# Handing out expert pages inside the graph network's loop, with scatters to fixed pages, in a graph and mixture kernel

## The reference, cut to what matters

```python
    xn = _layernorm(x, axis=-1)
    x = x + gnn(xn, edge_index, edge_attr_64, ...) + mix(xn, ...)
    z = _layernorm(x, axis=-1)
    # the experts, on z (256 wide; the hidden width H is 64)
    logits = z @ router_w.T + router_b
    idx = argmax(logits, axis=-1)
    h = relu(einsum('nd,ndh->nh', z, W1[idx]) + b1[idx])
    return x + relu(einsum('nh,nhd->nd', h, W2[idx]) + b2[idx])
```

## Time and profile before

| | |
|---|---|
| median of 3 runs | 2876.47 us |
| profiled execution, own time | 2884.98 us |
| its span, first to last instruction | 2883.2 us |
| mean granted TensorE clock | 0.956 |
| busy: TensorE, its weight loads | 2631.6 us (91%), 2462.9 us (85%) |
| busy: VectorE, ScalarE, POOL | 2143.3 us (74%), 1581.4 us (55%), 1756.9 us (61%) |
| moved by DMA | 207.99 MB, mean 72 GB/s |

### The profile page before, as it was taken

How to read it: one execution, slowest core, us unless ns; L and a number is a source line. 1 busy time by engine, 2 the same in 40 slices (tenths; PEclk the granted TensorE clock), 3 DMA queues, 4 the chain that set the end, 5 groups by cost and what they waited for, 6 DMA issues and landing times.

```text
span 2883.2 us, 57776 instructions
## 1 busy us (share of the span) xinstructions
PE 2631.6 (91%) x19546; PEld 2462.9 (85%) x19546; DVE 2143.3 (74%) x4892; ACT 1581.4 (55%) x3080; POOL 1756.9 (61%) x1614
## 2 busy tenths in 40 slices
PE   5889999999989999998999999899999998993497
PEld 3667899999989999997999999799899998993365
DVE  8988677777767777776777777788888886894055
ACT  0545476666636666664666666444444445671165
POOL 2045587777778777777877776555555553224566
PEclk7999999999999999999999999999999998996699
DMA  6022322222242232224222222343333322201343
GB/s 127 29 49 55 96 64 68 64 58 61 51 116 60 61 69 59 64 45 118 60 64 64 65 59 51 94 120 89 86 89 87 93 75 57 62 26 39 83 116 94
DMA packets 255570, 207.99 MB, mean 72 GB/s; under 512 B 165506, under 2 KB 194387, under 8 KB 255278
## 3 DMA queue, kind: packets, MB, share of 16 engines
q1 hardware_dynamic: 197678, 162.55, 21.8%
q0 software_dynamic: 57600, 41.75, 7.3%
HBM read 136.93 MB, written 70.16 MB: 72 GB/s over the span
## 4 chain that ended last, share of the span: by engine, by line
PE 59%; DVE 15%; POOL 11%; issue 9%; ACT 2%; DVEq 1%; DMA 1%; SPq 0%; ACTq 0%; POOLq 0%; another core or an unknown queue 0%
PE bank L399 54%; POOL edges_sorted L787 7%; PE bank L1918 4%; DVE hidh_lo L1394 3%; POOL tokens_sorted L853 2%; DVE xh L1358 2%; DVE scr L1268 1%; DVE oh L1591 1%; DVEq L1570 1%; PE bank L2381 1%; POOL ehl L803 1%; DVE bn L1349 1%; POOL r L765 1%; DMA queries<-qn 1%; DVE res L1366 1%
## 5 line engine op out<-in xcount | busy, mean ns | idle before, releaser
L787 POOL DMA_INDIRECT edges_sorted<-staging,pos_i x850 | 1075.7, 1265 | 246.4 <-issue 229.8
L910 ACT ACTIVATE hid<-bank,b1p 128x250 f32<-128x250 f32 x800 | 331.5, 466 | 319.3 <-PE bank L399 286.3
L399 PE MATMUL bank<-w_hi,hidh_hi 128*125 128x256 f32 x1600 | 472.2, 295 | 23.1 <-DVE hidh_lo L1394 22.9
L399 PE MATMUL bank<-h_hi,w_hi 128*128 128x250 f32 x1600 | 479.1, 299 | 3.7 <-DVE h_lo L1378 3.4
L399 PE MATMUL bank<-w_hi,hidh_lo 128*125 128x256 f32 x1600 | 453.7, 284 | 0.0
L1394 DVE TENSOR_TENSOR hidh_lo<-hid,hidh_hi 128x500 fp32r<-128x500 f32 x400 | 319.7, 800 | 178.6 <-ACT hidh_hi L916 145.7
L399 PE MATMUL bank<-w_lo,hidh_hi 128*125 128x256 f32 x1600 | 452.2, 283 | 0.0
L399 PE MATMUL bank<-h_hi,w_lo 128*128 128x250 f32 x1600 | 448.5, 280 | 0.0
L399 PE MATMUL bank<-h_lo,w_hi 128*128 128x250 f32 x1600 | 445.0, 278 | 0.0
L399 PEld LDWEIGHTS bank<-w_hi,hidh_hi 128*125 128x125 f32 x1600 | 300.8, 188 | 32.1 <-DVE hidh_lo L1394 29.3
L399 PEld LDWEIGHTS bank<-h_hi,w_hi 128*128 128x128 f32 x1600 | 303.9, 190 | 8.4 <-DVE h_lo L1378 6.1
(11 more groups left out here) (292 smaller groups left out, 6625.5 us busy)
## 6 DMA issues: line engine op xcount, KB each, us to landing
staging<-edges_sorted SPq DMA_DIRECT2D x103, 260.0 KB
staging<-in_edge_attr SPq DMA_DIRECT2D x50, 531.2 KB
queries<-qn SPq DMA_DIRECT2D x100, 250.0 KB
qin<-queries SPq DMA_DIRECT2D x100, 250.0 KB
edges_sorted<-staging,pos_i POOLq DMA_INDIRECT x850
rows_in<-edges_sorted SPq DMA_DIRECT2D x50, 260.0 KB
yin<-tokens_sorted SPq DMA_DIRECT2D x81, 127.0 KB
raw<-in_L_mix_W SPq DMA_DIRECT2D x8, 1024.0 KB, 5.6
```

The lines of the kernel that those rows point to most:

```text
L399: return nc.tensor.matmul(o, left, right, start=start, stop=stop, skip_group_check=True)
L787: nc.gpsimd.indirect_dma_start(out=edges_sorted, out_offset=bass.IndirectOffsetOnAxis(ap=pos_i[:, i:i + 1], axis=0), in_=stage[:, slot, j, ...
L910: a = nc.scalar.activation(hid[c % 2][:, j, :], chunks(PH[c % 2])[:, j, :], ACT.Gelu, bias=b1p[:, 2 * c + j:2 * c + j + 1])
```

## The change

The table of sorted tokens becomes 80 pages of 128 rows (`PAGE`), and each page belongs to one expert. Pages are handed out as the groups come: for every group the kernel counts how many tokens of each expert there are so far, opens a new page for an expert whose last one is full, and gives each token of the group a row. POOL scatters the group's two tiles at once, in the graph loop.

- `rank_tokens(g)` on TensorE, first in pass `g + 7`: three to five small products of `chosen` (now bf16, in two buffers) with triangles and ones, summed in `PQT` over all groups. It waits for `chosen` of the group, the last instruction of VectorE's pass before, and for `n_counted` of the group before.
- On VectorE nine instructions more for group `i-7` in pass `i`, between the others: `route_rank` (two), `route_pages` (two), `route_ends` (a scan), `route_grown`, `route_book`, `route_pick` (256 columns) and `route_sum` (a reduce over 320 columns). `route_count` and the old rank (four instructions) go.
- On POOL `token_slots(i-8)`, nine small instructions, and `scatter_tokens(i-8)`, two indirect DMAs, at the end of pass `i`. The loops become one pass longer on TensorE and VectorE, and four on POOL.
- Since rows of a page may stay unused, all 80 pages are written beforehand: in passes 0 to 19 of the first layer SP issues three transfers each (`fill_pages`), which put any finite values and the row number 25000 there, which the scatter of the results skips. They stand behind `load_queries` and ahead of what SP issues for the rest of the pass.
- The position arithmetic and the table of segments go. SP reads the experts of the pages back with one load (`page_kind`), and loads page after page from addresses fixed in the program, with no register. `omiss` goes. 24 idle products stand ahead of the expert loop, before its wait for the table.
- Buffers: the bf16 helpers of the edge sort (`tri16` and its like) lie in a place of `hid[1]` now. Two small memsets come to the set-up of constants, and five VectorE instructions in place of one ahead of the graph loop.

The diff, cut to its core:

```diff
-IDLE_SCATTER = 48
+IDLE_LOAD = 24
...
+PAGE = 128
+PAGE_RND = 8388608.0 * PAGE
+FILL = 4
+FSEGS = (N + EXP * (PAGE - 1)) // PAGE
...
-    tokens_sorted = nc.dram_tensor("tokens_sorted", (N, YROW), F32, kind="Internal").ap()
+    tokens_sorted = nc.dram_tensor("tokens_sorted", (FSEGS * PAGE, YROW), F32, kind="Internal").ap()
...
+        chosen = [sb(f"chosen{i}", [P, PAIR, EXP], BF16) for i in range(2)]
+        tri_r = sb("tri_r", [128, 128], BF16)
+        ones_r = sb("ones_r", [128, 128], BF16)
+        rest_r = sb("rest_r", [128, 128], BF16)
...
+            def fill_pages(t):
+                rows = tokens_sorted[t * FILL * PAGE:(t + 1) * FILL * PAGE, :].rearrange("(k p) c -> p k c", p=PAGE)
+                for k in range(KC):
+                    sp.dma_start(rows[:, :, k * 128:(k + 1) * 128], tri[:, :].unsqueeze(1).to_broadcast((PAGE, FILL, 128))).then_inc(blank_written, 16)
+                sp.dma_start(rows[:, :, D:YROW], unused[:, :].unsqueeze(1).to_broadcast((PAGE, FILL, YROW - D))).then_inc(blank_written, 16)
...
+                if l == 0 and t == 0:
+                    sp.wait_ge(consts, NCONST)
+                if l == 0 and 0 <= t < FSEGS // FILL:
+                    fill_pages(t)
...
-            sp.wait_ge(r_table, 2)
+            sp.dma_start(page_kind[:, :, :], tokens_sorted.rearrange("(k p) c -> p k c", p=PAGE)[0:1, :, D:YROW]).then_inc(blank_written, 16)
             for n in range(FSEGS):
-                first = sp.value_load(ffirst_i[0:1, n:n + 1], min_val=0, max_val=N - P)
                 if n >= YIN:
                     sp.wait_ge(f_row, n - YIN + 1)
-                    sp.wait_ge(f_idx, 2 * (n - YIN + 1))
-                sp.dma_start(yin[n % YIN][:, :], tokens_sorted[bass.ds(first, P), :]).then_inc(tokens_in(n)[0], 16)
+                    sp.wait_ge(f_idx, n - YIN + 1)
+                sp.dma_start(yin[n % YIN][:, :], tokens_sorted[n * PAGE:(n + 1) * PAGE, :]).then_inc(tokens_in(n)[0], 16)
...
+            nc.gpsimd.memset(unused[:, :], 0.0).then_inc(consts, 1)
+            pool.wait_ge(consts, 6)
+            nc.gpsimd.memset(unused[:, 2:3], float(4 * N)).then_inc(consts, 1)
...
+            def token_slots(g):
+                old, new = g % 2, (g + 1) % 2
+                pool.wait_ge(n_placed, g + 1)
+                of_kind = picked[:, g % 2, :, :]
+                rank, late, more = of_kind[:, :, 4], slots[:, 2, :], slots[:, 3, :]
+                for k in range(2):
+                    own_step(nc.gpsimd.tensor_tensor(slots[:, k, :], of_kind[:, :, 2 * k], of_kind[:, :, 2 * k + 1], ALU.subtract))
+                own_step(nc.gpsimd.tensor_tensor(late, rank, of_kind[:, :, 2 * old + 1], ALU.subtract))
+                pool.wait_ge(p_step, own[0])
...
+                own_step(nc.gpsimd.tensor_copy(fpos_i[:, PAIR * g:PAIR * (g + 1)], slots[:, 5, :]))
+                SLOTTED[g] = own[0]
+                pool.wait_ge(p_step, own[0])
+
+            def scatter_tokens(g):
+                for t in range(PAIR * g, PAIR * (g + 1)):
+                    nc.gpsimd.indirect_dma_start(
+                        out=tokens_sorted, out_offset=bass.IndirectOffsetOnAxis(ap=fpos_i[:, t:t + 1], axis=0),
+                        in_=res[:, t, :], in_offset=None).then_inc(f_scat, 16)
+
+            for i in range(GROUPS + 8):
                 if i < GROUPS:
                     pool.wait_ge(N_IN[i % 2], 16 * (i // 2 + 1))
                     nc.gpsimd.tensor_tensor(pair(res, i), pair(res, i), x_in[i % 2][:, :, :], ALU.add).then_inc(n_x, 1)
-                if i >= 4:
+                if 4 <= i < GROUPS + 4:
                     pool.wait_ge(n_ve, i - 3)
                     nc.gpsimd.tensor_tensor(pair(res, i - 4, D + 1)[:, :, D], gve[:, :], tail_half[:, :], ALU.pow).then_inc(n_root, 1)
-
-            pool.wait_ge(f_posi, 1)
-            for t in range(TILES):
-                nc.gpsimd.indirect_dma_start(
-                    out=tokens_sorted, out_offset=bass.IndirectOffsetOnAxis(ap=fpos_i[:, t:t + 1], axis=0),
-                    in_=res[:, t, :], in_offset=None).then_inc(f_scat, 16)
-                if t == TILES - 4:
-                    nc.gpsimd.memset(tail_half[:, :], -0.5).then_inc(f_ones, 1)
-
-            pool.wait_ge(f_scat, 16 * TILES)
+                if i == 8:
+                    pool.wait_ge(blank_written, 32 + 16 * (KC + 1) * (FSEGS // FILL))
+                if i >= 8:
+                    token_slots(i - 8)
+                    scatter_tokens(i - 8)
...
-            step_(nc.vector.memset(before_j[:, :, :, :], 0.0))
+            step_(nc.vector.tensor_copy(tri_r[:, :], tri[:, :]))
+            step_(nc.vector.tensor_copy(ones_r[:, :], ones[:, :]))
+            step_(nc.vector.tensor_tensor(rest_r[:, :], ones[:, :], tri[:, :], ALU.subtract))
+            step_(nc.vector.memset(book[:, :, :], 0.0))
+            step_(nc.vector.memset(ends[:, :, :], 0.0))
...
+                if g >= 2:
+                    dve.wait_ge(n_ranked, g)
+                nc.vector.tensor_tensor(chosen[g % 2][:, :, :], iota_seg[0:P, 0:EXP].unsqueeze(1).to_broadcast((P, PAIR, EXP)),
+                                        pair(res, g, D + 4)[:, :, D + 3:D + 4].to_broadcast((P, PAIR, EXP)), ALU.is_equal).then_inc(n_chosen, 1)
...
+            def book_of(g):
+                old, new = g % 2, (g + 1) % 2
+                return book[:, 2 * old, :], book[:, 2 * old + 1, :], book[:, 2 * new, :], book[:, 2 * new + 1, :]
 
             def route_rank(g):
-                stepped()
-                step_(nc.vector.tensor_reduce(frank[:, PAIR * g:PAIR * (g + 1)], rank_j[:, :, :], AX, ALU.add))
+                dve.wait_ge(n_ranked, g + 1)
+                step_(nc.vector.tensor_scalar(limits[:, :], PQT[0:P, PAIR * EXP:(PAIR + 1) * EXP], (PAGE - 1) / 2.0, PAGE_RND, ALU.add, ALU.add))
+                step_(nc.vector.tensor_tensor(picks[:, :, 4, :], PQT[0:P, 0:PAIR * EXP].rearrange("p (j e) -> p j e", j=PAIR),
+                                              chosen[g % 2][:, :, :], ALU.mult))
+
+            def route_pages(g):
+                end_old, held_old, end_new, held_new = book_of(g)
+                stepped()
+                nc.vector.tensor_scalar(held_new, limits[:, :], -PAGE_RND, None, ALU.add).then_inc(n_counted, 1)
+                step_(nc.vector.scalar_tensor_tensor(out=fresh[:, :], in0=limits[:, :], scalar=-PAGE_RND, in1=held_old, op0=ALU.add, op1=ALU.subtract))
+
+            def route_ends(g):
+                stepped()
+                step_(nc.vector.tensor_tensor_scan(ends[:, g % 2, :], ones[0:P, 0:EXP], fresh[:, :], ends[:, (g + 1) % 2, EXP - 1:EXP], ALU.mult, ALU.add))
+
+            def route_grown(g):
+                stepped()
+                step_(nc.vector.scalar_tensor_tensor(out=fresh[:, :], in0=fresh[:, :], scalar=0.0, in1=ends[:, g % 2, :], op0=ALU.is_gt, op1=ALU.mult))
+
+            def route_book(g):
+                end_old, held_old, end_new, held_new = book_of(g)
+                stepped()
+                step_(nc.vector.tensor_tensor(end_new, fresh[:, :], end_old, ALU.max))
+
+            def route_pick(g):
+                stepped()
+                dve.wait_ge(n_counted, COUNTED + g + 1)
+                step_(nc.vector.tensor_tensor(picks[:, :, 0:4, :], book[:, :, :].unsqueeze(1).to_broadcast((P, PAIR, 4, EXP)),
+                                              chosen[g % 2][:, :, :].unsqueeze(2).to_broadcast((P, PAIR, 4, EXP)), ALU.mult))
+
+            def route_sum(g):
+                stepped()
+                if g >= 2:
+                    dve.wait_ge(p_step, SLOTTED[g - 2])
+                nc.vector.tensor_reduce(picked[:, g % 2, :, :], picks[:, :, :, :], AX, ALU.add).then_inc(n_placed, 1)
...
-            for i in range(1, GROUPS + 6):
+            for i in range(1, GROUPS + 7):
...
+                if live(7):
+                    route_rank(i - 7)
                 if live(6):
                     route_logits(i - 6)
+                if live(7):
+                    route_pages(i - 7)
+                if live(6):
                     route_best(i - 6)
+                if live(7):
+                    route_ends(i - 7)
                 if live(1):
                     graph_low(i - 1)
+                if live(7):
+                    route_grown(i - 7)
                 if live(0):
                     graph_means(i)
+                if live(7):
+                    route_book(i - 7)
                 if live(6):
                     route_index(i - 6)
+                if live(7):
+                    route_pick(i - 7)
                 if live(2):
                     graph_hidden_low(i - 2, 1)
+                if live(7):
+                    route_sum(i - 7)
...
-            segment_counts(EXP, P, FSEGS, 1, PS)
-            segment_kinds(P, FSEGS, fkind, fkind_i, ffirst_i, 1, PS)
+
             for i in range(3):
-                nc.vector.memset(hsT[i][EH:EH + 1, :], 1.0).then_inc(f_bias, 1)
```

(22 more changed lines are left out.)

141 lines of the change are left out of this document (54 added, 87 removed).

## The result

The changed kernel takes 2934.55 us (median of 4 runs, 2926.33 to 2937.88); the kernel before had 2873.75 us in the median of its runs. The ratio is 1.0203, with an interval of 1.0167 to 1.0239: slower, by 61 us in the medians. The forecast was 2901, with a range up to 2926. So the sign was right and the size too small.

What follows compares the result with a forecast made beforehand. TensorE was taken as the bound, never idle in the graph loop. Loop loss 92.1, end gain 66.9, then -1.6, +0.5 and +0.8 made +24.9 us: 2901.4 against the median, range 2856 to 2926.

Steps and rivals of the forecast that it cites:

- ahead of the loop: Set-up ahead of the graph loop: five instructions ahead of the first means in place of one, 0.8 us.
- the ring: Graph loop: rank products wait for VectorE's `chosen` of the pass before, so a pass takes 11.55 us against 8.50.
- the clock: Graph loop: TensorE's 2.45 us idle per pass makes the granted clock fall, costing 1.6 us in each pass.
- POOL's add on the ring: POOL's add to `res` holding VectorE in the graph loop; no term in the forecast's sum, only a rival.
- end of the loop to the first page load: Position arithmetic goes and 48 of 50 scatters run under the loop: 38.1 us in place of 105.0, gain 66.9.
- expert part: Expert loop: 80 pages in place of 81 segments, -1.6 us; reading back the table of experts, 0.5.
- The fills: 60 fill transfers in SP's queue, passes 0 to 19 of the first layer: 0 us; sign if wrong, longer layer.
- That the scatters leave the end: Scatters move from the end into the graph loop, two per pass; their not leaving got no chance.
- 7.9 of 13 us, hidden: POOL in a graph-loop pass: slots 2.7 and two scatters 3.1 on top of 2.1 us, hidden.
- the third rival: POOL's add holds a VectorE chain instruction for 1.09 us, pass 14.27: +45.7, 2922.2 us; chance 0.14.
- long instructions behind the low parts: Sign of POOL's add meeting the chain: two-input VectorE instructions of over 1 us behind the low parts.
- grown, means, book or pick: VectorE instructions said to stand where POOL's add comes, some 8 us into a graph-loop pass.
- The rule: A VectorE instruction with two SBUF inputs and a GpSimd one reading SBUF exclude each other, first come first served.
- would be hit too: By the exclusion rule VectorE's new chain, mostly two-input instructions, would be held by POOL; no size in the sum.

Runs made afterwards that it cites:

- bare_ring: Changed kernel with POOL's add ahead of the slots and 14 idle TensorE products ahead of the rank products' wait: 2892.24 us in one run.
- add_first: Changed kernel with POOL's add of x for the next group moved ahead of slots and scatters: 2916.07 us, ratio to before 1.0129.
- late_rank: Changed kernel with TensorE's rank products moved from the head of the pass to behind its transposes: 2851.43 us, ratio to before 0.9903.
- late_and_add: Changed kernel with rank products behind the transposes and POOL's add ahead of the slots: 2835.33 us, ratio to before 0.9817.
- best: Both moves (rank products behind transposes, POOL's add first), plus two small VectorE instructions per pass taken once ahead of the loop: 2842.04 us, ratio 0.9825.
- scatter125: Changed kernel with the results' scatter taking 125 rows of each page instead of 128, leaving three out: 2930.65 us in one run.

## Why the prediction was right in sign and wrong in size

On the traced pair (+41.4) the steps stand thus; a gain has a minus.

| step | predicted | measured |
|---|---|---|
| ahead of the loop | 0.8 | 2.5 |
| the ring (3.05 a pass, with first and last pass) | 61.2 | 57.4 |
| the clock (1.63 a pass) | 31.0 | 40.2 |
| POOL's add on the ring | 0 | 22.7 |
| end of the loop to the first page load | -66.9 | -65.1 |
| expert part | -1.1 | -19.2 |
| behind the last product | 0 | 2.8 |
| sum | 24.9 | 41.4 |

Measured are the differences of the table of parts (loop 296.2 - 175.9 = 120.4 with the unrounded starts, split by bare_ring and add_first), the first router products (2436.87 - 2434.38), and what lies behind TensorE's last product (2924.6 - 2912.1 against 2883.2 - 2873.4).

**Right:** the closed ring, its length (11.30 for a forecast of 11.55), its releaser, and that the clock falls behind the gap. The end, within 2 us. The fills, whose price in the layers can't be told from nothing: the router starts 2.5 us later, and 6 us lie between two traces of before. That the scatters leave the end.

**The step that failed** is the one on POOL: "7.9 of 13 us, hidden". I asked whether POOL had the time, not what it would stop while it worked. The add came last in POOL's pass and met VectorE on the ring, 8.16 us into the pass: at the time that the third rival gave ("some 8 us into a pass") and near its price (1.1 a pass in the loop's sum; 1.33 with the clock kept up; the rival had 1.09). That rival got 0.14, on the ground that in half the passes the add falls where VectorE waits; but the pass of VectorE and that of POOL are locked by the ring, and an instruction stood still in each of the 16 passes. So it should have been a term of the forecast's sum. It was not right in all, though. What stood still was `held` or a low part of the hidden values, and not grown, means, book or pick: VectorE was not that far yet, and the rival's sign, long instructions behind the low parts, did not come. That the price fits is partly luck: 1.70 us (`held`) or 1.11 (the low part) were lost at the place, of which 1.1 to 1.35 reached the ring. Its 14.27 a pass stands near the measured 14.86 (the mean of the 16), but its +45.7 stands near the traced +41.4 because two errors cancel: the loop lost 120.4 where it had 92.1 + 19 x 1.09 = 112.8, and the expert part gave 18 more.

**The rule** that I weighed there, the Trainium skill's SBUF — State Buffer, section "Who interferes with whom", agrees with the rows: the low part and the scan have two inputs in SBUF and stood still for POOL's add. The same section lists the tensor-scalar operations among those that can take the shared ports in a mode of their own; `held`, with one input in SBUF, stood still as they did (1.87 against 0.17), though no row shows which mode it ran in. First come, first served is not what the recorded starts show: `held` began 0.52 us ahead of the add and was the one that waited. I wrote the new chain "would be hit too" and left it out of the sum.

**The clock's term** was mis-sized: 1.63 a pass from one fall of 3.4 us, measured 2.0. The price of a fall was right, and their number wrong. These are two passes of add_first, which has no add on the ring:

```profile
2513.30:2527.80 14.50, 12.21 (x79) 12.00 (x79) 8.09 (x33) 5.95 (x13) 6.06 (x13) 0.76 0.16 42
2527.80:2540.80 13.00, 10.57 (x80) 10.36 (x80) 8.15 (x35) 5.95 (x13) 6.06 (x13) 0.87 0.32 76
```

By its clock of 0.87 the second spent 3.4 us at half speed (13.0 x 0.13 x 2), and it is 1.6 longer than the ring of 11.30; the first, at 0.76, spent twice that and is 1.6 longer again. Six of 16 passes there are of the long kind, and after had 7.4 us at 0.50 in the window shown.

**The expert part** was read as 1.59 us a segment where the clock is full, and what the old loop lost beside that was not counted: the trace of before had it (9.9 us of idle TensorE and a granted clock of 0.92 in the window above; 158.2 us for 81 segments are 1.95 each). That the pages rid the loop of most of the idle time and part of the slow clock was not foreseen, and why is open. It hid part of the larger loss in the loop.

The time by the medians, +61, lies above what either traced pair shows, and above the range; the traces don't say where the other 20 us were, and the later run of after, at +38, doesn't have them.

## What to carry to other kernels

A wait placed at the head of an engine's pass closes a ring through whatever produces its value; the same work put behind the other products that VectorE needs early no longer held those up, and that turned this change from 2% slower to 1% faster (2% faster with the add moved as well). When work is put under a loop, ask of the engine that takes it not only whether it has the time, but which of its instructions now come at another moment, and what they stop there. A gap on TensorE once in every pass can be paid twice: for its length, and again in the clock behind it. Gaps of 2.4 to 3.7 us were; in late_rank, where TensorE is busy for 34.29 of 40 us and its one gap in a pass is 1.4 us, the clock stayed at 1.00.

## What the runs showed of the hardware that was not expected

- VectorE is held by a POOL instruction from before that one's recorded start. In late_rank the low part begins at 2506.86, the add at 2507.70, and the low part lasts 2.69 us instead of 0.67, so it stood for 0.8 us behind a scatter that held nothing in add_first (0.17 us for `held` at 2548.93 under the second scatter), nor a low part in late_and_add (0.67 us at 2500.37). The add waiting next in POOL's queue is what differs. Whether the add had begun before its recorded start the rows can't tell, since the profile gives spans on POOL only roughly.
- The victim changes with the place, and it need not be long: `held` on 32 columns (0.17 to 1.87), the scan (0.28 to 2.03), the low part (0.67 to 2.69), the shift on two columns (0.15 to 1.26).
- POOL is held by VectorE as well: in best the root takes 1.28 us instead of 0.73 where a low part runs beside it.
- An indirect DMA of 125 rows takes POOL 1.19 us, one of 128 rows 0.97 (scatter125 and after).
